# Attention of the last row in two parts of four tiles, with an expert stage of the row before between them

## The chip, the cores and the metric

The kernel runs on one core of one Trainium2 chip. The metric is the time on the device in microseconds (us). A core has five engines that run their own instruction streams and wait for each other through semaphores: TensorE (PE: matrix products into the eight PSUM banks; PEld is its weight load), VectorE (DVE), ScalarE (ACT), GpSimd (POOL) and SyncE (SP), which here only issues DMA transfers.

## The reference

Four rows of 1024 tokens with 128 features go through four residual steps, each behind a layer norm:

```python
x = x + attn_a(layernorm(x))   # linear attention within a token, 16 heads of 8, and a gelu MLP
x = x + ffn(layernorm(x))      # 32 experts of width 64, top 8 by a router
x = x + attn_b(layernorm(x))   # causal attention, 16 heads, window of 64 tokens, output product with bias
x = x + ffn(layernorm(x))      # the same experts again
```

The expert step, for all tokens and all 32 experts, is

```python
y = (x @ up.T) * silu(x @ gate.T) @ down.T      # per expert
acc += y * w_e[:, None]                          # w_e: weight of the token for this expert, 0 outside its top 8
```

and needs, before its first product is weighted, the router of its own input: logits, the top 8, their exponentials, and the division by their sum.

## The kernel before, in words

**Expert stages.** Every expert step of a row is done for two halves of 512 tokens, so a row has four expert stages, (row, 0) and (row, 1) before its windowed attention and (row, 2) and (row, 3) behind it. The code calls 512 tokens a group. A stage has 16 chunks (two experts each), and its 16 slots are the frame in which all else is placed. In slot s PE does `gate_up(s)` (six products of 128x512, L1353 to L1355, into one of three pairs of banks, called rings), and `down` of the chunk three slots earlier (L1378, two passes). Between them lie ACT's `silu` (L933), DVE's `gated` (L1158), and POOL's `hidden` (L776), which multiplies by the expert weights that a DMA has spread over the partitions (`spread_w`). PE runs three chunks ahead of its own `down` (`LAG`).

**Windowed attention.** It works on tiles of 128 tokens, eight in a row. A tile has scores in two pairs of head groups (`score`, L1392 and L1399, banks 0 to 3), the negative maxima (DVE `maxima`, L1185), the exponentials with their sums (ACT `exponentials`, L953), the reciprocals (DVE `invert`, L1193), the scaling (POOL `normalise`, L784), the transposes (`turn_probs`, L1414, banks 4 and 5), their copies (DVE `turned`, L1199), the product with the values (`mix`, L1428, bank 6), DVE `take_mix` (L1206) and POOL `pick` (L790, L792). The stages of the pipeline are spread over three tiles: PE does the scores of tile i, the transposes of tile i-1 and the mix of tile i-2. The first score of a tile is issued in slot 15 of the expert stage ahead, whose last three `down`s run inside attention, and `gate_up` of chunks 0 and 1 of the next stage run inside its last steps, ahead of the mixes of the last two tiles. Attention and expert chunks use the same banks, so apart from these ends they do not overlap.

**Order.** `SCHEDULE` is a list written by `stages_of`. Period p has the stages "first" (p, 0), "second" (p-1, 2), "third" (p, 1), "fourth" (p-1, 3) and then "attn" of row p with all eight tiles; period 0 has no "second" and "fourth", period 4 only these. So the end of the program is: first (3,0), second (2,2), third (3,1), fourth (2,3), attention of row 3, second (3,2), fourth (3,3). Everything smaller is a step with a slot, named in `PLAN` or, for one period, in `SPECIAL`: a slot of a stage, or one of the three hooks of each tile plus three at the end (slots 0 to 26 of "attn"). Every engine walks the same plan and does its part of each step, in this order and in no other. Steps that need PSUM outside the streams take turns in bank 7 (`SIDE_BANK`, `SIDE_AT`).

**What leads from attention to the expert stage behind it.** `proj(row, g)` is the output product of four tiles (L1326 and L1330, then a DVE add, L1101); it needs `pick` of the last of them. Then come, for stage (row, 2 + g): `m_stats` (DVE, L1009 and L1012), `m_rstd` (POOL, L732 to L735), `m_apply` (ACT, L834), `moe_turn` (PE L1251), `z_hi`, `z_lo` (L1113), `route` (PE L1283, L1285), `r_sum`, `top`, `weigh` (ACT, exponentials), `comb`, `cnorm`, `weighT` (PE L1293 and ACT L902). Then SP sends the weights to DRAM (`send_weights`, L582) and spreads them back in quarters (`spread_quarter`, L592); a quarter is loaded into a buffer that the quarter two before it has left. In rows 0 to 2 this chain for (row, 2) lies in the expert stages of the next period. In row 3 it lies in slots 17 to 25 of its own attention, and its weights are asked for there (`late`).

**What leads from the expert stage to attention.** For each group: `y_back` (the sum of the expert step turned back, PE L1300, DVE L1101), `s_stats`, `s_rstd`, `s_apply`, `seq_turn`, `keys` (L1307), `queries` (L1312) and `values` (L1319, ACT L925). SP writes the values to DRAM (`send_values`, L601) and reads them back in windows for two tiles at a time (`load_windows`, L608).

Of the kernel before, what the change touches and what calls it, by code (L numbers as in the profile page):

```python
# [29 lines left out]
T = 4  # L30
# [48 lines left out]
def back(*steps):  # L79
# [79 lines left out]
    },  # L159
}  # L160
# [162 lines left out]

def stages_of(period):
    if period < ROWS:
        yield "first", period, 0
    if period:
        yield "second", period - 1, G
    if period < ROWS:
        yield "third", period, 1  # L330
    if period:
        yield "fourth", period - 1, G + 1
    if period < ROWS:
        yield "attn", period, None
# [3 lines left out]
STREAM = [(row, f) for _, place, row, f in SCHEDULE if place != "attn"]  # L338
STAGE_AT = {stage: k for k, stage in enumerate(STREAM)}
STREAM_PERIOD = [period for period, place, _, _ in SCHEDULE if place != "attn"]  # L340
ENDS = {sum(p <= period for p in STREAM_PERIOD) - 1: period for period in range(ROWS)}
RINGS = {32: [0, 1, 2] * 4 + [1, 2] + [0, 1, 2] * 6, 64: ([0, 1, 2] * 6 + [1, 2]) * 2 + [0, 1, 2] * 8}
STARTS = [k for k, period in enumerate(STREAM_PERIOD) if k == 0 or STREAM_PERIOD[k - 1] != period]


def slot_steps(period, place, at):
    for name, n, rows in SPECIAL.get((period, place), PLAN[place]).get(at, []):
        if 0 <= period + rows < ROWS:
            yield period + rows, name, n


def slots_of(place):
    return range(HOOKS * TILES + 3) if place == "attn" else range(CH)
# [22 lines left out]
def hybrid_block(nc, x, wqkv_a, lam, g1, g2, g3, w1, w2, wqkv_b, wout, bout, wgate, wg, wu, wd, out):  # L376
# [3 lines left out]
    with ExitStack() as ctx:  # L380
# [139 lines left out]
        def attn_before(row, f):  # L520

            k = STAGE_AT[row, f]
            return STREAM_PERIOD[k] - 1 if k in STARTS and k else None

        def stream_end(row):

            return sum(period <= row for period in STREAM_PERIOD)

# [5 lines left out]
        def rings_of(row, f):  # L534
            return RINGS[CH * STREAM_PERIOD.count(STREAM_PERIOD[STAGE_AT[row, f]])]

# [25 lines left out]
        def _(sp):  # L562
# [67 lines left out]

            for period, place, row, f in SCHEDULE:
                late = period in (0, ROWS - 1)
                if place == "attn":
                    send_values(row, 1)
                    if period:
                        store_half(row - 1, 1)
                    load_windows(row, 2)
                    load_windows(row, 3)
                    if late:
                        next_weights(stream_end(row))  # L640
                    continue
# [6 lines left out]
                if period < ROWS and place == ("fourth" if period else "third"):  # L648
                    first_values(period)
# [9 lines left out]
        def _(pool):  # L659
# [135 lines left out]
            for period, place, row, f in SCHEDULE:  # L795
                if place != "attn":
# [3 lines left out]
                else:  # L800
                    for i in range(TILES):
                        normalise(row, i, 0)
                        run_steps(steps, period, place, HOOKS * i)
                        run_steps(steps, period, place, HOOKS * i + 1)
                        normalise(row, i, 1)
                        if i > 1:
                            pick(row, i - 2)
                        run_steps(steps, period, place, HOOKS * i + 2)
                    pick(row, TILES - 2)
                    pick(row, TILES - 1)  # L810
                    for last in range(3):
                        run_steps(steps, period, place, HOOKS * TILES + last)

        @block.scalar
        def _(act):
# [141 lines left out]
            for period, place, row, f in SCHEDULE:  # L957
                if place != "attn":
                    for s in range(CH):
                        if s == LAG and not starts_stream(row, f):  # L960
                            y_copy(STAGE_AT[row, f] - 1)
                        if s >= (FIRST if period == 0 else 1) or not starts_stream(row, f):
                            silu(row, f, s)
                        run_steps(steps, period, place, s)
                else:
                    exponentials(row, 0, 0)
                    exponentials(row, 0, 1)
                    for i in range(TILES):
                        exponentials(row, i, 2)
                        exponentials(row, i, 3)  # L970
                        if i == 0:
                            y_copy(stream_end(row) - 1)
                        run_steps(steps, period, place, HOOKS * i)
                        if i + 1 < TILES:
                            exponentials(row, i + 1, 0)
                        run_steps(steps, period, place, HOOKS * i + 1)
                        if i + 1 < TILES:
                            exponentials(row, i + 1, 1)
                        run_steps(steps, period, place, HOOKS * i + 2)
                    run_steps(steps, period, place, HOOKS * TILES)  # L980
                    silu(*STREAM[stream_end(row)], 0)
                    run_steps(steps, period, place, HOOKS * TILES + 1)
                    run_steps(steps, period, place, HOOKS * TILES + 2)
# [3 lines left out]
        def _(dve):  # L987
# [220 lines left out]
            for period, place, row, f in SCHEDULE:  # L1208
                if place != "attn":
# [301 lines left out]
```

## Time and profile before

| | us |
|---|---|
| three runs, median (lowest, highest) | 1052.81 (1051.34, 1057.58) |
| the profiled execution, its time | 1050.18 |
| its span | 1048.4 |
| mean granted clock of TensorE | 0.959 |
| busy PE, POOL, DVE, ACT | 938.2, 657.5, 646.9, 609.1 |

The profiled execution is one run of its own; 1.8 us of its time lie outside the span. The granted clock is 1 at 2.4 GHz and 0.5 at 1.2 GHz. In the page's 40 slices (26.2 us each) PE is at 9 tenths almost everywhere after the first eight slices; the exceptions are slices 35 to 37, which is where attention of row 3 lies:

```
PE   3246999889999999999999998999999999988998
PEclk9998999866899999999999999999999999988999
```

### The profile page before, as it was taken

The numbers are of one execution on the slowest core, as the hardware profiler recorded it, in microseconds if no ns is written. First come the engines' busy times: TensorE is split into PE (matmuls) and PEld (weight loads), VectorE is DVE, ScalarE is ACT, GpSimd is POOL, SyncE is SP. The second block draws the span as 40 slices with busy tenths as digits, with TensorE's granted clock in tenths as the row PEclk, the third lists the DMA queues.
The fourth block names the chain that finished last, engine by engine and source line by source line (L and its number), as shares of the span: only waits on it lengthen the run. The fifth ranks groups of instructions, "written<-read, shape, count | busy, mean of one in ns | idle before, by whom it ended". The sixth has DMA issues, their size and how long they took to land.

```text
span 1048.4 us, 16649 instructions
## 1 busy us (share of the span) xinstructions
PE 938.2 (89%) x5472; PEld 649.0 (62%) x5472; DVE 646.9 (62%) x1444; ACT 609.1 (58%) x1865; POOL 657.5 (63%) x607
## 2 busy tenths in 40 slices
PE   3246999889999999999999998999999999988998
PEld 1034665568666666668666665668666666676665
DVE  5884785447775864779737854779744343576432
ACT  4246565657366557689384566689364453875432
POOL 5763778444568874857668764857655645454654
PEclk9998999866899999999999999999999999988999
DMA  5004343101435543541234433541153555011652
GB/s 176 1 0 94 80 91 73 41 2 42 103 85 119 110 104 83 121 95 43 61 83 107 106 81 84 121 94 43 41 122 82 123 122 124 19 42 28 137 123 60
DMA packets 63224, 85.67 MB, mean 82 GB/s; under 512 B 3681, under 2 KB 29090, under 8 KB 62882
## 3 DMA queue, kind: packets, MB, share of 16 engines
q1 hardware_dynamic: 63138, 84.61, 35.8%
q8 instruction: 43, 0.70, 0.3%
q14 instruction: 43, 0.35, 0.1%
HBM read 79.32 MB, written 5.28 MB: 81 GB/s over the span
## 4 chain that ended last, share of the span: by engine, by line
PE 63%; ACT 12%; DVE 6%; POOL 6%; issue 5%; DMA 1%; DVEq 0%; SPq 0%; ACTq 0%; POOLq 0%
PE bank L1378 17%; PE bank L1353 8%; PE bank L1355 8%; PE bank L1354 8%; ACT probs L953 4%; PE bank L1414 4%; PE bank L1399 4%; PE bank L1428 2%; POOL work L776 2%; PE bank L1392 1%; PE bank L1251 1%; PE bank L1257 1%; ACT work L933 1%; ACT L933 1%; DVE probsT L1199 1%
## 5 line engine op out<-in xcount | busy, mean ns | idle before, releaser
L776 POOL TENSOR_TENSOR work<-work,spread_w 128x512 f32<-128x512 f32 x256 | 336.8, 1327 | 186.0 <-DVE work L1158 164.9
L1158 DVE TENSOR_TENSOR work<-work,bank 128x512 f32<-128x512 f32 x256 | 174.4, 682 | 242.4 <-ACT work L933 144.3
L1378 PE MATMUL bank<-work,down_w 128*128 128x512 f32 x512 | 265.3, 602 | 10.1 <-ACT yT L945 5.6
L933 ACT ACTIVATE work<-bank 128x512 f32<-128x512 f32 x256 | 150.8, 595 | 179.4 <-PE bank L1355 175.9
L953 ACT ACTIVATE probs<-bank,neg_max 128x96 f32<-128x96 f32 x512 | 165.7, 381 | 32.5 <-DVE neg_max L1185 19.9
L1353 PE MATMUL bank<-z_hi,gate_hi 128*128 128x512 f32 x256 | 171.9, 671 | 0.0
L784 POOL TENSOR_TENSOR probs<-probs,prob_inv 128x768 f32<-128x768 f32 x64 | 94.0, 1469 | 89.5 <-DVE prob_inv L1193 89.4
L953 ACT ACTIVATION_READ_ACCUMULATOR probs<-bank,neg_max 128x1 f32 x512 | 125.2, 248 | 0.0
L1378 PEld LDWEIGHTS bank<-work,down_w 128*128 128x128 f32 x512 | 95.8, 191 | 39.8 <-POOL work L776 11.3
L1355 PE MATMUL bank<-z_hi,gate_lo 128*128 128x512 f32 x256 | 102.6, 401 | 0.0
L1353 PE MATMUL bank<-z_hi,up_hi 128*128 128x512 f32 x256 | 102.2, 399 | 0.0
L1354 PE MATMUL bank<-z_lo,gate_hi 128*128 128x512 f32 x256 | 101.9, 398 | 0.0
L1355 PE MATMUL bank<-z_hi,up_lo 128*128 128x512 f32 x256 | 101.7, 397 | 0.0
L1354 PE MATMUL bank<-z_lo,up_hi 128*128 128x512 f32 x256 | 101.1, 395 | 0.0
L1199 DVE COPY probsT<-bank 96x512 f32<-96x512 f32 x128 | 81.6, 669 | 18.7 <-PE bank L1414 17.3
L743 POOL TENSOR_TENSOR kv_terms<-elu,qkv 128x1024 f32<-128x1024 f32 x32 | 83.5, 2613 | 10.2 <-DVE elu L1023 9.9
L1414 PE MATMUL bank<-ident,probs 128*96 128x128 f32 x512 | 80.1, 307 | 7.1 <-DVE probsT L1199 5.8
L1185 DVE TENSOR_REDUCE neg_max<-bank 128x4 f32<-128x384 f32 x128 | 64.9, 547 | 28.7 <-PE bank L1399 27.8
L1399 PE MATMUL bank<-keysT,qm 32*128 32x96 f32 x1024 | 76.1, 288 | 0.0
L1414 PEld LDWEIGHTS bank<-ident,probs 128*96 128x96 f32 x512 | 61.7, 140 | 20.4 <-issue 12.0
L1399 PEld LDWEIGHTS bank<-keysT,qm 32*128 32x128 f32 x1024 | 74.0, 207 | 0.0
L1353 PEld LDWEIGHTS bank<-z_hi,gate_hi 128*128 128x128 f32 x256 | 49.4, 193 | 38.3 <-issue 30.1
(142 smaller groups left out, 1467.3 us busy)
## 6 DMA issues: line engine op xcount, KB each, us to landing
spread_w<-comb_dram SPq DMA_DIRECT2D x128, 512.0 KB, 6.7
vals<-v_dram SPq DMA_DIRECT2D x16, 384.0 KB, 4.2
x_buf<-x SPq DMA_DIRECT2D x8, 256.0 KB, 3.3
v_dram<-v_tok SPq DMA_DIRECT2D x8, 256.0 KB, 6.7
out<-xs SPq DMA_DIRECT2D x8, 256.0 KB, 5.1
spread_w<-wg SPq DMA_DIRECT2D x1, 1024.0 KB, 6.4
spread_w<-wu SPq DMA_DIRECT2D x1, 1024.0 KB, 8.5
comb_dram<-combT SPq DMA_DIRECT2D x16, 64.0 KB, 1.6
```

The source lines that it names most:

```text
L776: pool.tensor_tensor(work[:, n % WORK], work[:, n % WORK], spread_w[:, n // EACH % 2, s % EACH], ALU.mult).then_inc(hid_gated, 1)
L784: pool.tensor_tensor(pr, pr, prob_inv[:, i % 2, part].unsqueeze(2).broadcast_to([P, HALF_BLOCKS, KW]), ALU.mult).then_inc(probs_normed, 1)
L933: act.activation(work[:, n % WORK], bank[GATE_BANKS[ring_of(row, f, s)]], ACT.Silu).then_inc(silu_ready, 1)
L953: a = act.activation(probs[:, i % 2, m], bank[hg][:, b * KW:(b + 1) * KW], ACT.Exp, bias=neg_max[:, i % 2, m:m + 1], accum_out=prob_sum[:, ...
L1158: dve.tensor_tensor(work[:, n % WORK], work[:, n % WORK], bank[UP_BANKS[ring_of(row, f, s)]], ALU.mult).then_inc(gated_ready, 1)
L1199: dve.tensor_copy(probsT[:, b], bank[4 + b % 2][0:KW, :]).then_inc(probsT_copied, 1)
L1353: pe.matmul(dst, w_hi[:, cols], h, start=True, stop=False)
L1354: pe.matmul(dst, w_hi[:, cols], l, start=False, stop=False)
L1355: pe.matmul(dst, w_lo[:, cols], h, start=False, stop=True).then_inc(ready, 1)
L1378: pe.matmul(bank[Y_BANK], down_w[:, c], work[:, n % WORK], start=(c == 0), stop=(c == CH - 1)).then_inc(down_done, 1)
L1399: mm = pe.matmul(bank[hg][:, KW * b:KW * (b + 1)], qm[feats, i // T, NB * (i % T) + b].rearrange("p j q -> p (j q)"), keysT[feats, first:f ...
L1414: mm = pe.transpose(bank[4 + b % 2][0:KW, P * hg:P * (hg + 1)], probs[:, i % 2, hg * NB + b], ident[:])
```

## The change

The last row's attention is split: period 3 becomes first (3,0), second (2,2), third (3,1), "attn_lo" (tiles 0 to 3 of row 3), fourth (2,3), "attn_hi" (tiles 4 to 7), and period 4 stays second (3,2), fourth (3,3). All loops over tiles run over the part's own range, with the ends (first score in slot 15, the three late `down`s, two early `gate_up`s, the two last mixes) kept for each part. The rings of banks are written out for stretches of 16, 32, 48 and 64 chunks. The steps of row 3 are placed anew: those towards attention of group 0 all in "third" (values in slot 9 rather than in slot 3 of "fourth"), `y_back(3,1)` and `s_stats(3,1)` in "attn_lo", and the rest of group 1 in "fourth", together with `proj(3,0)` and the whole chain of stage (3,2), which was in attention. `y_back(2,3)` is in slot 5 of "attn_hi". SP sends the values of group 1 and their windows in "fourth", and asks for the weights of (3,2) at its end.

```diff
+    "attn_lo": {
+        5: own(("y_back", 1)),
+        6: own(("s_stats", 1), ("s_rstd", 1)),
+    },
+    "attn_hi": {
+        5: back(("y_back", 3)),
+    },
...
-    (ROWS - 1, "attn"): {
-        8: back(("y_back", 3)),
-        17: own(("proj", 0), ("m_stats", 2), ("m_rstd", 2)),
-        18: own(("m_apply", 2)),
-        20: own(("moe_turn", 2), ("z_hi", 2)),
-        21: own(("z_lo", 2)),
-        22: own(("route", 2)),
-        23: own(("r_sum", 2), ("top", 2), ("weigh", 2)),
-        24: own(("comb", 2), ("cnorm", 2)),
-        25: own(("weighT", 2)),
-    },
+    (ROWS - 1, "third"): {
+        0: own(("seq_turn", 0)),
+        1: own(("keys", 0)),
...
+        5: back(("y_back", 2)) + own(("queries", 0)),
...
+        9: back(("top", 3)) + own(("values", 0)),
...
+        13: back(("weighT", 3)),
+    },
+    (ROWS - 1, "fourth"): {
+        0: own(("s_apply", 1)),
+        2: own(("seq_turn", 1)),
+        3: own(("proj", 0), ("m_stats", 2), ("m_rstd", 2)),
+        4: own(("keys", 1), ("m_apply", 2)),
+        6: own(("moe_turn", 2), ("z_hi", 2)),
+        7: own(("z_lo", 2)),
+        8: own(("route", 2), ("r_sum", 2)),
+        9: own(("top", 2), ("values", 1)),
+        10: own(("weigh", 2)),
+        11: own(("comb", 2), ("queries", 1)),
+        12: own(("cnorm", 2)),
+        13: own(("weighT", 2)),
+    },
...
+    elif period == ROWS - 1:
+        yield from (("first", period, 0), ("second", period - 1, G), ("third", period, 1),
+                    ("attn_lo", period, PARTS["attn_lo"]), ("fourth", period - 1, G + 1),
+                    ("attn_hi", period, PARTS["attn_hi"]))
...
-RINGS = {32: [0, 1, 2] * 4 + [1, 2] + [0, 1, 2] * 6, 64: ([0, 1, 2] * 6 + [1, 2]) * 2 + [0, 1, 2] * 8}
+RINGS = {16: [0, 1, 2, 1, 2, 0, 1, 2, 0, 1, 2, 1, 2, 0, 1, 2], 32: [0, 1, 2] * 4 + [1, 2] + [0, 1, 2] * 6,
+         48: [0, 1, 2] * 16, 64: ([0, 1, 2] * 6 + [1, 2]) * 2 + [0, 1, 2] * 8}
...
+FIRST_VALUES = {(0, "third"): 0, (1, "fourth"): 1, (2, "fourth"): 2, (ROWS - 1, "third"): ROWS - 1}
+LAST_VALUES = {(ROWS - 1, "fourth"): ROWS - 1}
...
-                if fg + 1 < len(STREAM) and not (late and fg + 1 == stream_end(period)):
+                if fg + 1 < len(STREAM) and not (period == 0 and fg + 1 == SEGMENT.count(0)):
                     next_weights(fg + 1)
...
                 else:
-                    end, following = stream_end(row) * CH, STREAM[stream_end(row)]
-                    for i in range(TILES):
+                    end, following = END_AT[row, f[0]] * CH, STREAM[END_AT[row, f[0]]]
+                    for i in range(*f):
+                        at = HOOKS * (i - f[0])
                         score(row, i, (2, 3))
-                        if i == 0:
+                        if i == f[0]:
                             down(end - 3)
```

## Rows read from the trace of the kernel before

**Rows 1.** The page, part 4: the chain that ended last, shares by engine.

```profile
PE 63%; ACT 12%; DVE 6%; POOL 6%; issue 5%; DMA 1%; DVEq 0%; SPq 0%; ACTq 0%; POOLq 0%
```

**Rows 2.** Busy time by stretch; first score to first `down` behind attention, rows 3, 2, 1.

```profile
core 0: us, PE busy (x) PEld busy (x) DVE busy (x) ACT busy (x) POOL busy (x), PEclk, DMA share, GB/s
896.28:974.82 78.54, 68.83 (x751) 52.94 (x750) 51.82 (x124) 53.23 (x279) 37.82 (x40) 0.89 0.18 41
683.48:744.68 61.20, 57.87 (x725) 45.15 (x724) 48.59 (x105) 49.26 (x266) 36.61 (x35) 1.00 0.25 58
448.85:510.07 61.22, 57.91 (x725) 45.16 (x725) 48.55 (x105) 49.27 (x266) 36.57 (x35) 1.00 0.27 62
```

**Rows 3.** Timeline of PE in attention of row 3: start, us, engine, line, [idle before <-releaser].

```profile
937.22 2.04 PE L1326 MATMUL bank<-bout_row,ones_row 1*128 1x512 f32 x2 [3.37 <-POOL mixT L792]
...
964.93 1.91 PE L1414 MATMUL bank<-ident,probs 128*96 128x128 f32 x8 [2.71 <-DVE probsT L1199]
...
974.82 1.12 PE L1378 MATMUL bank<-work,down_w 128*128 128x512 f32 x2
```

**Rows 4.** The chain of waits at the end of that attention: start, us, what.

```profile
966.23 7.18 DMA spread_w<-comb_dram
```

**Rows 5.** The chain of waits, slot 14 of third (3,1); below, timeline of PE, slot 13.

```profile
855.14 0.86 PE bank L1378 x2
...
852.63 1.12 PE L1312 MATMUL bank<-seqT,qkv_b_w 128*128 128x512 f32 x2 [0.72 <-ACTq L904]
```

**Rows 6.** Timeline of PE in attention of row 2: scores of tiles 3 and 7, proj, mix.

```profile
704.94 0.33 PE L1392 MATMUL bank<-window,same_query 32*128 32x384 bf16 x2
...
726.41 0.38 PE L1392 MATMUL bank<-window,same_query 32*128 32x384 bf16 x2
...
738.05 1.12 PE L1326 MATMUL bank<-bout_row,ones_row 1*128 1x512 f32 x2
...
740.19 1.08 PE L1428 MATMUL bank<-probsT,vals 96*32 96x128 f32 x32
```

**Rows 7.** Timeline of DVE and of POOL at the end of attention of row 2.

```profile
737.69 1.28 DVE L1199 COPY probsT<-bank 96x512 f32<-96x512 f32 x2 [0.27 <-PE bank L1414]
...
742.93 0.46 POOL L792 TENSOR_TENSOR mixT<-mix_all 128x128 f32<-128x128 f32 x1
```

**Rows 8.** Timeline of DVE: `m_stats` of stage (3,2), inside attention of row 3.

```profile
942.31 0.87 DVE L1009 BATCH_NORM_STATS2 stats<-xs 128x6 f32<-128x128 f32 x4 [0.24 <-DVE xs L1101]
943.22 0.38 DVE L1012 BATCH_NORM_AGGREGATE moments<-stats 128x2 f32<-128x6 f32 x4
```

**Rows 9.** The chain of waits in expert stages: `down`s in successive slots, and `values`.

```profile
979.59 0.86 PE bank L1378 x2
981.83 0.86 PE bank L1378 x2
984.51 0.86 PE bank L1378 x2
986.75 0.86 PE bank L1378 x2
989.89 0.86 PE bank L1378 x2
...
867.24 0.89 PE bank L1319 x8
```

**Rows 10.** Timeline of ACT where attention of row 3 begins.

```profile
898.40 0.60 ACT L933 ACTIVATE work<-bank 128x512 f32<-128x512 f32 x1 [1.43 <-PE bank L1355]
899.02 1.28 ACT L953 ACT_TABLE_LOAD   x1
```

**Rows 11.** Busy time and granted clock (PEclk) by stretch, columns as in rows 2.

```profile
240.50:243.50 3.00, 2.73 (x49) 1.90 (x47) 2.77 (x7) 3.00 (x20) 2.26 (x3) 1.00 0.04 9
244.00:267.00 23.00, 22.91 (x185) 18.91 (x184) 16.48 (x45) 13.76 (x82) 9.98 (x10) 0.50 0.06 16
937.00:946.00 9.00, 8.78 (x64) 6.40 (x65) 2.96 (x12) 1.93 (x13) 2.14 (x6) 0.50 0.01 2
```

More of the change, by code:

```diff
@@ L321 @@
     ("lead", 1), ("lead", 2))
+PARTS = {"attn": (0, TILES), "attn_lo": (0, T), "attn_hi": (T, TILES)}
 def stages_of(period):
[L325 to L334, printed above, removed]
+    if period == 0:
+        yield from (("first", 0, 0), ("third", 0, 1), ("attn", 0, PARTS["attn"]))
+    elif period < ROWS - 1:
+        yield from (("first", period, 0), ("second", period - 1, G), ("third", period, 1),
+                    ("fourth", period - 1, G + 1), ("attn", period, PARTS["attn"]))
+    elif period == ROWS - 1:
+        yield from (("first", period, 0), ("second", period - 1, G), ("third", period, 1),
+                    ("attn_lo", period, PARTS["attn_lo"]), ("fourth", period - 1, G + 1),
+                    ("attn_hi", period, PARTS["attn_hi"]))
+    else:
+        yield from (("second", period - 1, G), ("fourth", period - 1, G + 1))
@@ L337 @@
 SCHEDULE = [(period, place, row, f) for period in range(ROWS + 1) for place, row, f in stages_of(period)]
[L338 removed]
+STREAM = [(row, f) for _, place, row, f in SCHEDULE if place not in PARTS]
 STAGE_AT = {stage: k for k, stage in enumerate(STREAM)}
[L340 to L342 removed]
@@ L346, in slot_steps @@
+STARTS = [k for k, part in enumerate(SEGMENT) if k == 0 or SEGMENT[k - 1] != part]
+FIRST_VALUES = {(0, "third"): 0, (1, "fourth"): 1, (2, "fourth"): 2, (ROWS - 1, "third"): ROWS - 1}
+LAST_VALUES = {(ROWS - 1, "fourth"): ROWS - 1}
 def slot_steps(period, place, at):
-    for name, n, rows in SPECIAL.get((period, place), PLAN[place]).get(at, []):
+    plan = SPECIAL[period, place] if (period, place) in SPECIAL else PLAN[place]
+    for name, n, rows in plan.get(at, []):
         if 0 <= period + rows < ROWS:
@@ L352, in slots_of @@
 def slots_of(place):
-    return range(HOOKS * TILES + 3) if place == "attn" else range(CH)
+    if place not in PARTS:
+        return range(CH)
+    first, end = PARTS[place]
+    return range(HOOKS * (end - first) + 3)
 def every_step():
@@ L522, in attn_before @@
             k = STAGE_AT[row, f]
-            return STREAM_PERIOD[k] - 1 if k in STARTS and k else None
-        def stream_end(row):
-            return sum(period <= row for period in STREAM_PERIOD)
+            return ATTN[SEGMENT[k] - 1] if k in STARTS and k else None
         def position(row, f, s):
@@ L961, in _ @@
                             y_copy(STAGE_AT[row, f] - 1)
-                        if s >= (FIRST if period == 0 else 1) or not starts_stream(row, f):
+                        if s >= (1 if STAGE_AT[row, f] else FIRST) or not starts_stream(row, f):
                             silu(row, f, s)
@@ L1434, in _ @@
             for period, place, row, f in SCHEDULE:
-                if place != "attn":
+                if place not in PARTS:
                     for s in range(CH):
-                        begun = starts_stream(row, f) and s < (EARLY if period else FIRST)
+                        begun = starts_stream(row, f) and s < (EARLY if STAGE_AT[row, f] else FIRST)
                         if s == CH - 1 and STAGE_AT[row, f] in ENDS:
-                            score(ENDS[STAGE_AT[row, f]], 0, (0, 1))
+                            score(*ENDS[STAGE_AT[row, f]], (0, 1))
                         if not begun:
@@ L1465, in _ @@
                     gate_up(*following, 0)
[L1466 removed]
+                    mix(row, f[1] - 2)
                     gate_up(*following, 1)
[L1468 to L1473 removed]
+                    run_steps(steps, period, place, drain)
@@ L1474, in _ @@
+                    turn_probs(row, f[1] - 1, (0, 1))
+                    run_steps(steps, period, place, drain + 1)
+                    turn_probs(row, f[1] - 1, (2, 3))
+                    run_steps(steps, period, place, drain + 2)
+                    mix(row, f[1] - 1)
             for n in range(ROWS * MOE * CH - LAG, ROWS * MOE * CH):
```

180 lines of the change are left out of this document (101 added, 79 removed).

## The prediction

> **What bounds the kernel now.** I read the chain of waits by engine first: 63% of it is PE, and all else is small [rows 1]. So time is to be had only where PE is not the last link. The 40 slices name the place, attention of row 3. Next I compared three stretches that hold the same work, from the first score to the first `down` of the stage behind attention: 78.54 us in row 3, 61.20 in row 2, 61.22 in row 1 [rows 2]. Up to tile 4 row 3 keeps the pace of row 2; the excess of 17.34 us comes later. The timeline of PE shows it: `proj(3,0)` waits 3.37 us for POOL's `mixT` and then takes twice its time, the transposes of the last tile begin after 2.71 us of idleness, also at half speed, and the first `down` comes at 974.82 [rows 3]. Its releaser is the weights of stage (3,2), whose spreading takes 7.18 us on the chain [rows 4]. Router, weights and DMA of (3,2) are squeezed into an attention that has nothing to hide them. The change gives them a whole expert stage as cover, and pays with a second start and end of the attention pipeline.
>
> **The sum, on PE's time.** Both kernels are compared from the end of slot 14 of "third" (3,1), at 855.14 + 0.86 = 856.00 [rows 5] (the score of slot 15 follows in the new kernel), to the first `down` of (3,2). In the kernel before these are 974.82 - 856.00 = 118.82 us.
>
> *Third.* `values(3,0)` comes in, 0.89 [rows 9]. `queries(3,0)` goes from slot 13 to 5; with it goes the wait of 0.72 behind `weighT` for bank 7 [rows 5]. The ACT copies that go along lie beside a PE that is full. Together +0.17.
>
> *attn_lo.* Row 2's stretch less four tiles. From the scores of tile 3 to those of tile 7 it is 726.41 - 704.94 = 21.47 [rows 6], so 61.20 - 21.47 = 39.73 for four tiles with full start and end. Three corrections. (a) `proj` is no longer in the end: in row 2 it holds PE from 738.05 to 740.19, where `mix` of tile 7 follows, while the copies that this mix needs were done at 737.69 + 1.28 = 738.97 [rows 6, 7]; so -1.22 (bounds: -2.14, all of proj; 0, if mix finds another wait). (b) `y_back(3,1)` takes the place of row 2's `y_back`, three slots earlier, but `s_stats(3,1)` comes on top: 0.87 + 0.38 = 1.25 on DVE [rows 8], which is busy for 48.59 of row 2's 61.20 us [rows 2], with its free time at the start and the end. Queued behind them on DVE are the maxima of tile 3, and ACT's exponentials wait for those. I take all of it, +1.25 (bounds: 0, absorbed while ACT catches up; 2.1, with the add of y_back too). `s_rstd` on POOL lies between two normalisations and is free unless POOL becomes late. (c) `seq_turn` in slot 2 of "fourth", four transposes: a slot with such transposes is 984.51 - 981.83 = 2.68 against 981.83 - 979.59 = 2.24, so +0.44 [rows 9]. Sum 40.20.
>
> *fourth, from its first `down` to the end of slot 14.* The `down` 0.86; `proj(3,0)` 2.14; eleven slots of 2.24, 24.64; `keys` and `queries`, two passes of a 128x512 product like `down`, 0.86 each; `values` 0.89; `moe_turn` and `weighT` 0.44 each; `route` 989.89 - 986.75 - 2.24 = 0.90 [rows 9]. `queries` in slot 11, four copies on ACT, stands right ahead of `cnorm`, for which `weighT` waits; the nearest row is the 0.72 of the same bank and the same two steps in "third" [rows 5]: I take 0.4, bounds 0 and 0.72. DVE's, ACT's and POOL's parts of the (3,2) chain lie under a PE that is full; slots 4 to 6 are the tightest, but `down` of a chunk comes three slots (6.7 us) behind it. The ring of 16 makes `gate_up(3)` wait for `gated(1)`, two chunks back rather than three; DVE has nothing ahead of that in slot 0, so 0 (bound 0.65). Sum 32.43.
>
> *attn_hi.* 39.73 again. `proj` of the first half is out, but `proj(3,1)` in slot 2 of "second" stands ahead of the first `down`. In row 2 the last `pick` ends at 742.93 + 0.46 = 743.39 [rows 7], 1.22 earlier without proj: 742.17. Then proj 2.14 and `gate_up(3)`, 2.24 - 0.86 = 1.38: the `down` at 745.69 on row 2's clock, against 744.68, so +1.01. Sum 40.74.
>
> *Queues.* SP sends `values(3,1)` behind the last quarter of (2,3) and waits for their landing, then loads two windows, then asks for (3,2)'s weights. That wait falls in slots 9 to 13, and the weights are wanted a whole attn_hi later. The windows of tiles 4 to 7 come before attn_hi begins. The weights of (2,3) gain attn_lo as cover. Storing row 2's last half goes from one attention to the next, far from the end. POOL's `m_rstd` and the picks lie where rows 0 to 2 have them. All 0; were the cover gone, SP's one late quarter would cost up to the 7.18 of [rows 4].
>
> In all 0.17 + 40.20 + 32.43 + 40.74 = 113.54, that is 5.3 us less than 118.82. The rest, second and fourth of period 4, is untouched. The profiled execution took 1050.18 us, so it becomes 1044.9; its time stands 2.6 below the median of the three runs, 1052.81, and against that the kernel comes to **1047.5**. With the bounds of (a), (b), the wait and the ring, 1045 to 1050.5.
>
> **A rule on the tables of ScalarE.** Each part of attention loads the table for exponentials once and silu loads its own back; with `weigh(3,2)`, which now falls among silus, that is four more loads. Where attention begins, silu starts at 898.40, takes 0.60, and the load starts at 899.02 and takes 1.28 [rows 10]: nothing lies between, and the 1.28 is inside the 39.73 of each part. The Trainium skill (ScalarE: Activation LUTs, "Table sets: the hidden batching unit" and "What ACT_TABLE_LOAD costs") speaks against the change: group by table set, since each switch costs the load of about 1283 ns and a drain of about 1380 ns. The row agrees with the load and shows no drain. By that rule the one added switch at the start of a part would cost 1.4 us more, an estimate from that page, and the sum would be 1048.9.
>
> **Rivals.** *The clock falls in the added ends (slower).* The place is the start and end of the two short parts: row 2's end has small holes of PE, (a) makes one of them longer, and (b) opens one in mid-attention. The granted clock is 0.50, the 1.2 GHz level, from 937.00 to 946.00 after the long idleness, and PE is busy for 8.78 of these 9 us, half of it lost: 4.4 us a fall [rows 11]. That a long idleness isn't needed shows in row 0: PE was busy for 2.73 of the 3.00 us from 240.50 to 243.50, in attention alone, and then ran at 0.50 for 23 us [rows 11]. Against it: attention of rows 1 and 2 ran at 1.00 throughout [rows 2]. The Trainium skill has this as a mode of its own (TensorE: Matmul & The Clock Gate, "A second HAM failure mode: psum-queue depth-cycling"): short idle spells between groups of matmuls are enough to make the clock swing between its levels. By that rule row 1 and 2 are luck; the rows bear it out for row 0 only. One fall gives 1047.5 + 4.4 = 1051.9, no change to speak of; from the second on the kernel is slower than before, 1056.3.
>
> *The second start and end cost nothing (faster).* Then the whole excess of 17.34 goes, but for the work that was in it and stays: proj(3,1) 2.14, route 0.90, two times 0.44; 13.4, so 1039.4. For it: DVE, ACT and PE are each below full at the ends, and moved steps could fill them. Against it: 4.6 slots of experts in a part of 39.73 us leave 29.4 for four tiles of 5.37, which is 7.9 us of filling and draining (less proj and y_back) twice, and nothing in the diff lets chunks run into it.
>
> *The weights of (3,2) are still late.* The chain could slip if `proj(3,0)` in slot 3 came late; but row 2's pick was done before its first `down`, and attn_hi is 40 us of cover. It would have to slip by all of this to be seen: 1052.8. I give it next to nothing.
>
> **How the numbers follow.** The forecast 0.51; one fall of the clock 0.18; two or more 0.12; more gain than my bounds 0.18; late weights 0.01. The range for 8 in 10 reaches from 1041, which leaves out most of the full gain, to 1056.5, which takes in two falls. About 1% (10.5 us) is what a measurement can tell from no change: below 1042.3 lies most of the "costs nothing" case, 0.15; above 1063.3 it takes three falls or more, 0.04; within, 0.81.
>
> **What would show it.** Step by step: from attn_lo's first score to the first `down` of (2,3) about 39.8 without `seq_turn`; the 16 slots of "fourth" with no PE wait over 1 us; `combT` of (3,2) sent before attn_hi; from attn_hi's first score to the first `down` of (3,2) 40.7, with POOL waiting for DVE there and not for `spread_w`. (b) is wrong if ACT has no new wait for `neg_max` in tile 3. The forecast is wrong if PEclk shows 0.50 in either part (then the first rival), or if a part takes under 36 us (then the second).

## The result, and the profile after

The changed kernel takes 1045.8 us (median of 20 runs, 1036.23 to 1049.83), the kernel before 1050.8 (20 runs, 1046.65 to 1057.58): ratio 0.9938, 95% interval [0.9915, 0.9961]. That is 5.0 us less by the medians, where 5.3 were forecast; a gain, but within 1%. The time itself was forecast as 1047.5, which is 1.7 too high, because it was set against the median of three runs, 1052.81, and 20 runs of the kernel before have 1050.8. Four of the changed kernel's 20 runs took 1036 to 1038 us at a mean granted clock of 0.974 or 0.975, the others 1041 to 1050 at 0.963 to 0.970. The profiled execution took 1046.79 us, its span 1045.1, mean granted clock 0.965.

The page's part 2 and the shares of its part 4, for the kernel after:

```profile
PE   3246899889999999999999998999999998999998
...
PEclk9998999866899999999999999999999999999999
...
PE 62%; ACT 13%; POOL 6%; DVE 5%; issue 5%; DMA 1%; DVEq 0%; SPq 0%; ACTq 0%; POOLq 0%
```

Before, slices 36 and 37 stood at 8 tenths, for PE and for its clock (slice 35, which is named with them ahead of the prediction, stood at 9). Now they are at 9, and slice 34, where attn_lo lies, is at 8. The chain is what it was, mostly PE [rows 1]. What the change brought has to be read by stretch. Busy time of the kernel after, in this order: third (3,1) from the `down` in slot 1 to that in slot 14; attn_lo from its first score to the first `down` behind it; fourth (2,3) from there to the first score of attn_hi; attn_hi likewise (us; busy time and count of PE, PEld, DVE, ACT and POOL; granted clock, DMA share, GB/s):

```profile
821.35:858.18 36.83, 34.46 (x138) 23.15 (x137) 14.43 (x41) 18.79 (x37) 19.58 (x18) 1.00 0.55 122
859.13:899.50 40.37, 36.73 (x383) 27.07 (x382) 25.83 (x58) 29.22 (x141) 21.87 (x24) 0.96 0.25 54
899.50:931.78 32.28, 32.28 (x130) 21.21 (x130) 13.59 (x40) 16.82 (x33) 18.06 (x17) 1.00 0.45 100
931.78:971.57 39.79, 36.39 (x390) 26.69 (x390) 25.68 (x52) 26.98 (x136) 22.44 (x21) 1.00 0.28 61
```

Before, the same `down`s of slot 1 and 14 stand at 820.86 and 854.98 (34.12), and the first `down` of (3,2) at 974.82 [rows 3]: 153.96 us from slot 1. After it is 971.57 - 821.35 = 150.22, so 3.74 less in the two profiles, and the spans differ by 3.3. Nearly the whole difference lies in this stretch. But its parts don't match the forecast: third took 2.71 more (forecast 0.17), the parts of attention 40.37 and 39.79 (40.20 and 40.74), fourth 32.28 (32.43). And attn_lo holds a short fall of the clock (0.96).

### The profile page after: what moved, and what is told of

It reads as the page before. It is cut to its first block, busy times and chain, and to the rows that moved or that the text cites. A ratio compares the mean times of both kernels' runs of the same rounds, so it can differ in the third digit from the quotient of the medians.

```text
span 1045.1 us, 16655 instructions
## 1 busy us (share of the span) xinstructions
PE 935.6 (90%) x5472; PEld 644.6 (62%) x5472; DVE 647.1 (62%) x1444; ACT 613.9 (59%) x1869; POOL 657.6 (63%) x607
## 4 chain that ended last, share of the span: by engine, by line
PE 62%; ACT 13%; POOL 6%; DVE 5%; issue 5%; DMA 1%; DVEq 0%; SPq 0%; ACTq 0%; POOLq 0%
PE bank L1432 16%; PE bank L1406 8%; PE bank L1408 8%; PE bank L1407 8%; ACT probs L1002 5%; PE bank L1468 4%; PE bank L1453 4%; PE bank L1482 2%; POOL work L824 2%; PE bank L1446 1%; PE bank L1304 1%; PE bank L1310 1%; DVE probsT L1250 1%; ACT work L982 1%; ACT L982 1%
## 5 line engine op out<-in xcount | busy, mean ns | idle before, releaser
L1209 DVE TENSOR_TENSOR work<-work,bank 128x512 f32<-128x512 f32 x256 | 174.2, 682 | 232.2 <-ACT work L982 145.4
L982 ACT ACTIVATE work<-bank 128x512 f32<-128x512 f32 x256 | 150.8, 595 | 184.2 <-PE bank L1408 181.3
L1406 PE MATMUL bank<-z_hi,gate_hi 128*128 128x512 f32 x256 | 169.3, 661 | 0.0
```

The source lines that it names most:

```text
L982: act.activation(work[:, n % WORK], bank[GATE_BANKS[ring_of(row, f, s)]], ACT.Silu).then_inc(silu_ready, 1)
L1209: dve.tensor_tensor(work[:, n % WORK], work[:, n % WORK], bank[UP_BANKS[ring_of(row, f, s)]], ALU.mult).then_inc(gated_ready, 1)
L1406: pe.matmul(dst, w_hi[:, cols], h, start=True, stop=False)
```

## The experiments

All stretches below are cut as above, so that kernels are compared by the work, not by the clock of an early stage.

**Is it the cover or the split?** The attention stays whole, and the chain of (3,2) goes into the expert stage ahead of it. This isn't usable as it is: `m_stats(3,2)` reads the rows before `proj(3,0)` has been added, so stage (3,2) is computed from its input without the attention of row 3. It is a bound for a chain with full cover and no second start and end.

```diff
     (ROWS - 1, "attn"): {
         8: back(("y_back", 3)),
-        17: own(("proj", 0), ("m_stats", 2), ("m_rstd", 2)),
...
-        25: own(("weighT", 2)),
+        26: own(("proj", 0)),
     },
+    (ROWS - 1, "fourth"): {
+        3: own(("values", 0), ("m_stats", 2), ("m_rstd", 2)),
...
+        13: own(("weighT", 2)),
+        14: own(("values", 1)),
+    },
...
-                late = period in (0, ROWS - 1)
+                late = period == 0
...
-                    dve.wait_ge(attn_b_done, group(row, n - G) + 1)
+                    dve.wait_ge(attn_b_done, group(row, n - G) + 1 - (G if (row, n) == (ROWS - 1, G) else 0))
```

> The kernel before, unsplit, with one part of the change alone: the whole chain of stage (3,2), m_stats to weighT and the asking for its weights, lies in fourth (2,3), as in periods 1 and 2. So that it can, m_stats(3,2) reads what xs holds before the last attention (the output half of row 2): stage (3,2) computes on other data, all else is the same work. My theory (the chain is squeezed, the split pays with a second start and end): attention of row 3 from the first score to the first down falls from 78.54 to row 2's 61.2 plus 2.1 for proj(3,1), about 63.3; the fourth stage grows by 2.2 (route 0.9, two times 0.44, up to 0.5 of waiting); the kernel is about 13 us faster than before, and about 8 us faster than the changed kernel, which is the price of the second start and end. PEclk in attention of row 3 stays 1.00. Rival (the second start and end cost nothing, the expected gain is simply not there because the chain was not what bound attention): the gain over the kernel before is about that of the change, 3 to 5 us.

Measured: 1039.12 us, ratio 0.9883 [0.9847, 0.9919]. Its attention, first score to first `down`:

```profile
897.61:961.05 63.44, 59.92 (x736) 46.46 (x736) 46.64 (x96) 48.63 (x265) 37.83 (x37) 1.00 0.23 56
```

That is row 2's 61.20 [rows 2] and one proj of 2.14, as expected. From slot 1 of third (819.03) it is 142.02 us, 11.94 less than before, with the clock at 1.00 in the attention. The excess of row 3's attention was the missing cover, and it goes when cover is there. The change keeps 3.74 of these 11.94 in its first profile and 5.22 in its second (below). The expected distance to the changed kernel, 8 us, was met in the first (8.20), but it isn't the price of the second start and end, as was expected: the next two experiments find 4.1 us of it elsewhere.

**Where third loses its time.** Timeline of the kernel after: PE, ACT and DVE in slots 4 to 6 of third (3,1).

```profile
832.03 0.60 PE L1353 MATMUL bank<-ident,yT 128*128 128x128 f32 x4
834.64 1.12 PE L1365 MATMUL bank<-seqT,qkv_b_w 128*128 128x512 f32 x2 [2.01 <-DVEq L1155]
...
838.37 0.63 PE L1304 MATMUL bank<-ident,z 128*128 128x128 f32 x4 [0.36 <-ACT qm L967]
...
831.87 0.86 ACT L883 ACTIVATE z<-xs,shift,rstd 128x128 f32<-128x128 f32 x2
832.64 0.57 ACT L982 ACTIVATE work<-bank 128x512 f32<-128x512 f32 x1
...
833.25 0.69 DVE L1209 TENSOR_TENSOR work<-work,bank 128x512 f32<-128x512 f32 x1 [3.36 <-ACT work L982]
833.85 0.68 DVE L1152 TENSOR_TENSOR xs<-xs,bank 128x512 f32<-128x512 f32 x1
```

Read it backwards. `queries(3,0)` (L1365) wants bank 7, which `y_back(2,2)` has just filled (L1353). The add that empties it (L1152) has its input at 832.6, but stands on DVE behind the `gated` of its chunk (L1209); this waits for ACT's `silu` (L982), and `silu` stands behind `m_apply` (L883), whose first part waited for POOL (`m_rstd`) until 831.09. PE pays 2.01 for it, and 0.36 more where the next user of bank 7 waits for the copies of `queries`. One line is changed:

```diff
-        3: back(("m_stats", 3), ("m_rstd", 3)),
+        3: back(("m_stats", 3), ("m_rstd", 3)) + own(("queries", 0)),
         4: back(("m_apply", 3)),
-        5: back(("y_back", 2)) + own(("queries", 0)),
+        5: back(("y_back", 2)),
```

> The changed kernel with queries(3,0) in slot 3 of third instead of slot 5, where y_back(2,2) stands right ahead of it for bank 7 and PE waits 2.01 us for DVE's add of y_back, and then 0.36 for the ACT copies of queries. Theory (the change lost 2.4 us by this one slot): in third there is no wait of PE over 0.5 us between slots 2 and 6, the stretch from the down of slot 0 to that of slot 14 is about 2.4 us shorter, and the kernel about 2.4 us faster than the changed one. Rival (ACT is the bound there, since four copies of 2.42 us stand before m_apply of stage (2,3)): the wait turns up at moe_turn in slot 6 and the gain is under 1 us.

Measured: 1042.15 us, ratio 0.991 [0.9876, 0.9945]. Third takes 34.01 (821.19 to 855.20), 2.82 less, where 2.4 were expected from the two waits; attn_lo takes 38.88, with no fall of the clock. In its timeline `queries` runs without a wait:

```profile
827.38 1.02 PE L1365 MATMUL bank<-seqT,qkv_b_w 128*128 128x512 f32 x2
```

**The stats in mid-attention.** `s_stats(3,1)` and `s_rstd(3,1)` move to slot 11 of attn_lo, behind the last maxima.

```diff
     "attn_lo": {
         5: own(("y_back", 1)),
-        6: own(("s_stats", 1), ("s_rstd", 1)),
+        11: own(("s_stats", 1), ("s_rstd", 1)),
     },
```

> The changed kernel with s_stats(3,1) and s_rstd(3,1) in slot 11 of attn_lo (last tile) instead of slot 6. In the changed kernel the DVE part delays the maxima of tile 3 (ACT waits 1.27 us for them), POOL's rstd stands before a normalisation, PE has holes of 0.59, 0.28 and 0.50 us and the clock falls for 3.4 us. Theory (my step b, and the holes bring the fall): attn_lo from first score to first down falls from 40.4 to 38.5 to 39, no stretch of it at 0.50. Rival (the step is absorbed, the end of the part is bound by PE's own order): under 0.4 us less, and the clock may fall all the same.

Measured: 1043.96 us, ratio 0.9927 [0.99, 0.9954]. Attn_lo of this kernel, and below it the same stretch of the changed kernel run again, where the clock did not fall (next experiment but one):

```profile
859.40:896.99 37.59, 34.80 (x384) 25.79 (x383) 25.75 (x58) 29.27 (x141) 21.89 (x24) 1.00 0.26 58
```

```profile
858.13:897.02 38.89, 35.24 (x384) 25.74 (x383) 25.84 (x58) 29.10 (x141) 21.88 (x24) 1.00 0.25 56
```

1.30 for two DVE instructions of 0.86 + 0.38, all of it on the path. How it gets there, DVE and ACT of the kernel after in tile 3:

```profile
879.20 0.86 DVE L1060 BATCH_NORM_STATS2 stats<-x_buf 128x6 f32<-128x128 f32 x4
880.10 0.38 DVE L1063 BATCH_NORM_AGGREGATE moments<-stats 128x2 f32<-128x6 f32 x4
...
880.97 1.01 DVE L1236 TENSOR_REDUCE neg_max<-bank 128x4 f32<-128x384 f32 x2
...
881.55 0.34 ACT L1002 ACTIVATE probs<-bank,neg_max 128x96 f32<-128x96 f32 x1 [1.27 <-DVE neg_max L1236]
```

ACT waits 1.27 for the maxima queued behind the stats, as the prediction's (b) has it. The part came out below the 38.5 to 39 expected, since from the 40.37 of the first profile both the stats (1.30) and the fall of the clock (1.48) went. That the holes of the stats bring the fall isn't shown by this run, since the kernel with these holes also ran without one.

**Both moves.** The edits of the last two together.

> The changed kernel with both moves, queries(3,0) in slot 3 of third and s_stats(3,1) in slot 11 of attn_lo. Theory: the two gains add, 3.5 to 4.5 us less than the changed kernel in the sum of third and attn_lo, about 9 us less than the kernel before. Rival (a wait is only passed on): no better than the better of the two alone.

Measured: 1041.73 us, ratio 0.9889 [0.9835, 0.9943]. Attn_lo, fourth, attn_hi:

```profile
857.27:894.85 37.58, 34.79 (x383) 25.79 (x382) 25.75 (x57) 29.27 (x141) 21.89 (x24) 1.00 0.27 58
894.85:927.12 32.27, 32.27 (x129) 21.21 (x131) 13.61 (x40) 16.83 (x33) 18.05 (x17) 1.00 0.44 100
927.12:966.95 39.83, 36.38 (x390) 26.70 (x390) 25.68 (x52) 27.05 (x136) 22.45 (x21) 1.00 0.29 61
```

From slot 1 of third (822.30) to 966.95 it is 144.65, 9.31 less than before, and 4.09 less than the changed kernel without a fall: the two savings add up.

**The change once more**, for the fall of the clock; nothing is edited.

> The changed kernel once more, as it is. In its first profile the clock fell for 3.4 us in attn_lo, at 40.37 us from first score to first down; the variant with queries(3,0) moved has the same attn_lo instruction by instruction, showed no fall, and took 38.88. Theory (the holes that s_stats opens make a fall possible, not certain: the fall costs 1.5 us and comes in some executions): attn_lo is either 38.9 with PEclk 1.00 or about 40.4 with a fall in it, nothing between; third's stretch from the down of slot 1 to that of slot 14 is 36.83 again. Rival (the fall belongs to the changed kernel's order): 40.4 again.

Measured: 1044.35 us, ratio 0.9932 [0.9904, 0.996]. Slot 1 of third to first `down` of (3,2) is 969.09 - 820.35 = 148.74, so 5.22 less than before; third is 36.83 again, with a wait of 2.02 in place of 2.01. Attn_lo shows the same small holes as in the first profile, but the clock stayed at 1.00 and the part took 38.89 (858.13 to 897.02); fourth took 32.28 again. So the fall doesn't belong to the order of the kernel.

**Is splitting of use without the excess?** The kernel with both moves, and row 2 split as well; its (2,2) chain stood in covered expert stages already.

```diff
+    (2, "third"): {
+        **PLAN["third"],
+        2: ahead(("h_red1", 0)) + own(("queries", 0)),
+        13: back(("weighT", 3)),
+        15: own(("values", 0)) + ahead(("expo", 1)),
+    },
+    (2, "fourth"): {
+        0: ahead(("mlp2", 0), ("elu", 1), ("attend", 4)) + own(("s_apply", 1)),
...
+        12: ahead(("cnorm", 0)) + own(("queries", 1)) + ahead(("wred", 6)),
...
-    elif period == ROWS - 1:
+    elif period in (2, ROWS - 1):
...
```

> The kernel of both moves, with attention of row 2 split in the same way too (four tiles, fourth (1,3), four tiles); nothing of a stage behind it gains cover there, since row 2's weights for (3,0) were in time already. So it adds one second start and end and nothing else, beside the moves of row 2's steps that the split needs. From the kernel of early weights (unsplit, 142.0 us from the down of slot 1 of third (3,1) to the first down of (3,2)) and that of both moves (split, 144.65) I work the price out as 144.65 - 142.0 + 0.72 + 0.99 for two waits that the unsplit one has, 4.4 us. Theory: slower than the kernel of both moves by 4 to 7 us (row 2's fourth stage is full of steps of row 3, so some more may be lost there). Rival (a start and end are free, PE fills them): within 1 us.

Measured: 1049.7 us, ratio 0.9981 [0.9953, 1.0009]. From the first `down` behind attention of row 1 to the first behind that of row 2 it takes 241.03 us (511.36 to 752.39), against 233.10 with both moves alone (513.03 to 746.13): 7.93 more, just above the 4 to 7 expected. Its two parts for row 2:

```profile
636.75:681.69 44.94, 39.47 (x399) 29.21 (x399) 27.70 (x63) 32.42 (x147) 21.90 (x23) 0.92 0.35 79
714.85:752.39 37.54, 34.34 (x379) 25.40 (x378) 28.24 (x61) 27.60 (x137) 21.30 (x20) 1.00 0.29 65
```

The second part is as short as attn_lo of row 3. The first is 7.4 longer, and its timeline of PE names why:

```profile
645.71 0.49 PE L1470 MATMUL bank<-window,same_query 32*128 32x384 bf16 x1 [2.24 <-ACT probs L1026]
647.00 0.49 PE L1470 MATMUL bank<-window,same_query 32*128 32x384 bf16 x1 [0.79 <-ACT probs L1026]
...
656.00 0.33 PE L1470 MATMUL bank<-window,same_query 32*128 32x384 bf16 x1 [0.86 <-ACT probs L1026]
```

Here `elu` of the next row stands on ACT ahead of the first exponentials, with a table load of its own, and the clock falls behind these waits (0.92 over the part). So this run shows that a split with nothing to cover gives nothing; how much of the 7.93 is the split and how much my placing of the next row's steps, it doesn't say.

**Split, but the chain of (3,2) back in attention**, in slots 1 to 9 of attn_hi.

```diff
     "attn_hi": {
-        5: back(("y_back", 3)),
+        1: own(("proj", 0), ("m_stats", 2), ("m_rstd", 2)),
+        2: own(("m_apply", 2)),
+        4: own(("moe_turn", 2), ("z_hi", 2)),
+        5: own(("z_lo", 2)) + back(("y_back", 3)),
+        6: own(("route", 2)),
+        7: own(("r_sum", 2), ("top", 2), ("weigh", 2)),
+        8: own(("comb", 2), ("cnorm", 2)),
+        9: own(("weighT", 2)),
     },
...
     (ROWS - 1, "fourth"): {
...
-        3: own(("proj", 0), ("m_stats", 2), ("m_rstd", 2)),
...
-        13: own(("weighT", 2)),
```

> The kernel of both moves with one part of the change undone: proj(3,0) and the whole chain of (3,2) are in slots 1 to 9 of attn_hi rather than in fourth (2,3), and its weights are asked for only then. The split stays. Theory (what the expert stage gives is cover on DVE, ACT and PE at once): fourth gets shorter by PE's part, 2.1 + 0.9 + 0.9 = 3.9, attn_hi longer by more than that, since its tiles keep DVE and ACT full and the chain has some 5 us for each: attn_hi 46 to 50 against 39.8, in sum 3 to 6 us slower than the kernel of both moves. Rival (only the time of the weights matters, any place before the end of attention does): attn_hi grows by no more than the 3.9, the sum is the same within 1 us.

Measured: 1059.11 us, ratio 1.0079 [1.0048, 1.011]; attn_hi:

```profile
911.94:975.30 63.36, 53.03 (x415) 40.12 (x415) 31.37 (x79) 31.43 (x150) 24.17 (x25) 0.73 0.19 39
```

and in it POOL, then PE:

```profile
926.38 0.23 POOL L780 TENSOR_SCALAR var_eps<-moments 128x4 f32<-128x4 f32 x1 [5.93 <-DVE moments L1063]
...
929.81 1.94 PE L1468 MATMUL bank<-ident,probs 128*96 128x128 f32 x8 [4.71 <-POOL probs L832]
...
939.43 1.09 PE L1353 MATMUL bank<-ident,yT 128*128 128x128 f32 x4 [2.84 <-DVE z_lo L1164]
```

`rstd` stands on POOL ahead of the normalisation, waits there 5.93 for the moments, and PE waits 4.71 for the normalised tile. From within this hole on, the clock is at 0.50 for 34 us (928 to 962). That is more than either theory had, 3 to 6 us or nothing: they counted waits, not a fall of this length. From slot 1 of third (811.02) to 975.30 it is 164.28, 19.63 more than with both moves, and this profile is of the fastest of its ten runs. The split with the chain inside is worse than the kernel before. How much of the 19.63 is the missing cover as such, how much these slots and how much the clock, the run doesn't say.

**proj(3,1) behind the first `down` of (3,2).** On top of both moves.

```diff
     (ROWS, "second"): {
-        2: back(("proj", 1), ("m_stats", 3), ("m_rstd", 3)),
+        3: back(("proj", 1), ("m_stats", 3), ("m_rstd", 3)),
```

> The kernel of both moves with proj(3,1) and the statistics of (3,3) in slot 3 of second (3,2) instead of slot 2, behind the first down as in rows 0 to 2. In the kernel of both moves PE waits 0.66 us for the last pick ahead of this proj. Theory: PE does gate_up(3) and waits for the first down instead, so the first down comes about 2.2 us earlier and the second one is level or up to 0.7 earlier; the kernel is the same to 0.7 us faster. Rival (m_apply in slot 4 now comes late and holds up silu): a new wait of PE in slots 6 to 8 and up to 2 us slower.

Measured: 1037.68 us, ratio 0.9862 [0.982, 0.9905]. From slot 1 of third to the second `down` of (3,2) it takes 146.84 us (816.12 to 962.96), against 146.89 (822.30 to 969.19) with the two moves: level, as expected. PE's wait for the last `pick` (0.66) is replaced by one for `hidden`:

```profile
958.46 1.12 PE L1432 MATMUL bank<-work,down_w 128*128 128x512 f32 x2 [0.45 <-POOL work L824]
```

**Whole or split, side by side.** The last two were measured together: the whole attention of the first experiment (again with stage (3,2) computed without the attention of row 3) with `proj(3,1)` in slot 3, and the split kernel with the three moves once more.

> The undivided attention of the early-weights kernel, with proj(3,1) in slot 3 of the stage behind it rather than slot 2. Theory (the second start and end of attention costs 4.4 us, whatever is tidied around it): the stretch from slot 1 of third (3,1) to the second down of (3,2) stays about 2.5 to 3 us shorter than in the split kernel with all three moves beside it, so its median lies 2 to 3 us below that one's, near ratio 0.984. Rival (the medians are ruled by falls of TensorE's clock in row 0, which neither kernel touches): the two medians lie within 1 us, either order, though the stretch differs by the 2.5 to 3 us.

> The split kernel with three moves (queries in slot 3 of third, s_stats in slot 11 of attn_lo, proj(3,1) in slot 3 of second) once more, with more rounds. Theory (the proj move is level in this stretch; its lead of 4 us over the kernel with two moves was few runs and the clock of row 0): ratio to the kernel before near 0.989. Rival (the proj move gives something that the stretch does not show): ratio near 0.986 again.

Measured: 1038.96 us, ratio 0.9886 [0.9864, 0.9908], for the whole one; 1038.91, ratio 0.9869 [0.9839, 0.9898], for the split one. The stretch differs by 2.63 us as the theory has it: 964.00 - 819.71 = 144.29 whole, 968.79 - 821.87 = 146.92 split. The medians don't show it: the rival named for the first of the two holds for them. The single runs show more. All six of the whole kernel had a granted clock of 0.965 to 0.968 and took 1035.12 to 1042.47. Of the split kernel's six, three had 0.964 or 0.965 and took 1040.46 to 1041.79; the other three had 0.967 to 0.980 and took 1032.52 to 1037.37. So the level medians come from a higher clock in some runs of the split kernel. Why the whole one had none of these isn't shown. The ratio of the split kernel, 0.9869, is nearer to its rival's 0.986 than to the 0.989 of the theory, and its interval holds both.

Where such differences arise is seen in the profiles, in attention of rows 0 and 1, which neither kernel touches; whole first, then split:

```profile
228.00:276.00 48.00, 47.01 (x460) 37.98 (x458) 31.15 (x74) 26.93 (x142) 20.13 (x21) 0.71 0.22 50
460.00:500.00 40.00, 38.72 (x567) 32.46 (x567) 35.03 (x75) 37.88 (x218) 27.37 (x27) 1.00 0.11 29
```

```profile
228.00:276.00 48.00, 45.83 (x480) 36.75 (x479) 34.11 (x85) 27.62 (x144) 22.69 (x25) 0.81 0.27 63
460.00:500.00 40.00, 39.38 (x533) 32.94 (x530) 33.11 (x70) 34.30 (x201) 24.76 (x24) 0.87 0.10 28
```

0.10 of the clock over 48 us is 4.8 us of full speed, and 0.13 over 40 us is 5.2, by this estimate each more than the difference sought; here they go against each other.

## Why the prediction was right, and where its steps were not

**The mechanism holds.** (3,2)'s router and weights had no cover; with cover, attention of row 3 falls to the pace of row 2 (the first experiment, 63.44), and with the chain back inside it, in the slots tried, nothing is won (the seventh).

**That the sum fits so closely is luck: its errors cancel.** Against the profile of the change in which the clock didn't fall, -5.22 measured and -5.3 forecast (attn_hi is from the other profile):

| term | forecast | measured |
|---|---|---|
| third, slots 1 to 14, more than before | 0.17 | 2.71 |
| attn_lo | 40.20 | 38.89 |
| fourth | 32.43 | 32.28 |
| attn_hi | 40.74 | 39.79 |

*Third* is the step that failed. The prediction moved `queries` from slot 13 to 5, took away the wait of 0.72 [rows 5], and named for it only the ACT copies "beside a PE that is full". Bank 7 had another user in slot 5. It asked who waits in slot 13, but not who holds the bank in slot 5, nor what stands ahead of the releasing add on DVE. It cost 2.82, by the second experiment; with `queries` in slot 3, third is at 34.01, within 0.3 of the forecast.

*The two parts of attention* are 1.31 and 0.95 shorter than forecast, for two reasons that they share and a third in attn_lo. The first is the place of `y_back`. The prediction saw it "three slots earlier" and took the 61.20 of row 2 over with no change for it. In row 2 PE waits for ACT's exponentials in the middle of the scores of tile 2, until 699.22, and later spends its own time on `y_back` (first block: before, chain of waits, then timeline of PE). In the kernel of both moves `y_back` fills that very place, and the scores behind it don't wait (second block, timeline of PE):

```profile
697.55 1.62 ACT probs L953 x10
699.22 0.33 PE bank L1392
...
704.41 0.60 PE L1300 MATMUL bank<-ident,yT 128*128 128x128 f32 x4
```

```profile
872.47 0.60 PE L1353 MATMUL bank<-ident,yT 128*128 128x128 f32 x4
873.00 0.34 PE L1446 MATMUL bank<-window,same_query 32*128 32x384 bf16 x2
...
878.30 0.53 PE L1446 MATMUL bank<-window,same_query 32*128 32x384 bf16 x2
```

From the first score to the scores of tile 3 row 2 takes 704.94 - 683.48 = 21.46 [rows 2, 6], attn_lo 878.30 - 857.27 = 21.03, and attn_hi of the kernel after 952.80 - 931.78 = 21.02: 0.43 less in each.

The second reason is in (a), the missing proj. The prediction let `mix` of the last tile start when the copies end. It begins 0.93 before that and only its last eight products wait for the last copy, here in attn_hi of the kernel after, in the chain of waits and then in the timeline of PE:

```profile
964.15 0.50 DVE probsT L1250
...
964.75 0.69 DVE probsT L1250
...
965.49 0.47 PE bank L1482 x8
```

```profile
964.51 1.41 PE L1482 MATMUL bank<-probsT,vals 96*32 96x128 f32 x32
```

Row 2 hid all this under its proj, so that the end of its copies, 738.97, was no bound for the start of `mix`. From the scores of the last tile to the end of the last `pick` attn_hi takes 968.02 - 952.80 = 15.22 and row 2 743.39 - 726.41 = 16.98 [rows 6, 7]: 1.76 less, where (a) had 1.22. These 0.54 and the 0.43 of `y_back` are the whole miss of attn_hi, 0.95, within 0.02.

*(c)*, the `seq_turn`, was taken at 0.44 and is all but hidden. Row 2's first `down` waits 0.47 for POOL's `hidden`; in the kernel of both moves `seq_turn` runs on PE in that time, and the `down` doesn't wait:

```profile
744.68 1.12 PE L1378 MATMUL bank<-work,down_w 128*128 128x512 f32 x2 [0.47 <-POOL work L776]
```

```profile
892.85 0.60 PE L1304 MATMUL bank<-ident,z 128*128 128x128 f32 x4
...
894.85 1.12 PE L1432 MATMUL bank<-work,down_w 128*128 128x512 f32 x2
```

From the scores of tile 3 to the first `down` attn_lo takes 894.85 - 878.30 = 16.55 and row 2 744.68 - 726.41 = 18.27: 1.72 less, where (a) and (c) together had 0.78. These 0.94 and the 0.43 of `y_back` are the miss of attn_lo, but for the 0.05 of (b).

*(b)* was taken at 1.25 and measured at 1.30 (third experiment), by the path named. *Fourth* was right within 0.15: PE is busy for 32.28 of 32.28 us, so the 0.4 for `weighT` was not to be paid, and the 0 taken for the ring was right. *Queues:* no releaser of a first `down` is `spread_w` any more; the late weights of the third rival don't occur.

**The first rival, the clock,** did occur in one profile of the change and not in the other, whose attention has the same holes. The stretch behind the holes in the first:

```profile
885.50:889.00 3.50, 3.42 (x13) 2.98 (x14) 2.49 (x5) 2.85 (x11) 2.96 (x3) 0.52 0.02 5
```

It lasted some 3.4 us and cost 40.37 - 38.89 = 1.48, not the 4.4 of a fall as long as that of before. So the place was right, the price a third, and it is not certain in a run. The prediction's sign for this rival, the clock at 0.50 in either part, was therefore too strict: it showed in the first profile, and the time still fell by what was forecast. **The second rival,** that the second start and end cost nothing, is refuted: the split kernel with its moves tidied (144.65) stands 2.63 above the whole one (142.02), although the whole one still has two waits of PE that the other has not (0.72 and 0.99, both at bank 7); without them the second start and end would be about 4.3, which is an estimate. It may be more, as the whole one has its `y_back` in slot 8, where it fills no wait. The forecast had 8.1 between its own sum and a free one (1047.5 and 1039.4), about twice that.

**The rule on ScalarE's tables** would have made the sum 1048.9. In attn_hi, 39.79, the parts found above (y_back, the copies) account for the miss within 0.02, so no added 1.4 is to be seen, although the program has the four more loads that were forecast (68, before 64); and where the table goes back to silu, in the kernel after, the load follows the last exponential at once:

```profile
886.52 0.29 ACT L1002 ACTIVATION_READ_ACCUMULATOR probs<-bank,neg_max 128x1 f32 x1
886.83 1.28 ACT L982 ACT_TABLE_LOAD   x1
```

**The best version** is the split with `queries(3,0)` in slot 3 and `s_stats(3,1)` in slot 11; with `proj(3,1)` in slot 3 too it had ratios of 0.9862 and 0.9869 in two series. The third move is level in the stretch, so its lead over the two moves (0.9889 [0.9835, 0.9943]) is not shown to be its own. The change as given leaves about 4.1 us of its possible gain in two places: 2.82 in slot 5 of third, 1.30 in slot 6 of attn_lo.

## What to carry to other kernels

A stage that must be computed out of the end of a pipeline is worth moving under full work even at the price of draining the pipeline once more: cover gave 11.9 us, and the second start and end took 2.6 of it back (with its steps placed well), or some 4 by the estimate above. When a step that takes turns at a shared PSUM bank is moved, look up who holds the bank in the new slot, and what stands in that releaser's queue ahead of it; here one line of a table, two slots off, took 2.8 of the 9.3 us that the better placement reaches. And a start or end without its filler must be timed from what the last product waits for, block by block, not from the filled version. Last, when a sum fits, compare it term by term: this one had 2.5 too little in one term and 2.4 too much in the others.

## What the runs showed of the hardware

The granted clock is not decided by the holes alone: attn_lo of the same kernel with the same waits (0.59, 0.17, 0.28 and 0.50 us in the first profile) ran once at 0.52 for some 3.5 us and once at 1.00. With a hole of 4.71 us it fell and stayed at 0.50 for 34 us, although PE was busy for 30.34 of the 34.00 us behind the hole (the seventh experiment):

```profile
929.80:963.80 34.00, 30.34 (x236) 25.15 (x240) 17.87 (x47) 17.97 (x93) 11.06 (x10) 0.53 0.04 11
```

And the falls in attention of rows 0 and 1 differ from profile to profile of kernels that are alike there (0.71 and 0.81 over the same 48 us, 1.00 and 0.87 over the same 40); they make kernels within 2 or 3 us of each other hard to order by the median. A stretch between two marks of the same work with no fall in it repeats to 0.1 us (36.83 twice, 146.84 and 146.92).
